# The maxima of the 64-wide attention heads, taken from the high halves of queries and keys as products on half of the array's rows

## The reference

```python
q = (x @ Wq).reshape(b, n, heads, -1)      # 16 heads of 64
k = (ctx @ Wk).reshape(b, j, heads, -1)    # j = 1601 rows of context
v = (ctx @ Wv).reshape(b, j, heads, -1)
sim = jnp.einsum('bihd,bjhd->bhij', q, k) * scale
attn = jax.nn.softmax(sim, axis=-1)
out = jnp.einsum('bhij,bjhd->bihd', attn, v).reshape(b, n, -1)
return out @ Wo + bo
```

## Time and profile before

| | |
|---|---|
| runs | 6561.17, 6562.08, 6566.58 us; median 6562.08 |
| profiled execution | 6568.9 us span, first to last instruction |
| TensorE busy | 6072.1 us, 92% |
| VectorE busy | 4851.4 us, 74% |
| ScalarE busy | 4175.0 us, 64% |
| GpSimd busy | 2747.1 us, 42% |
| mean granted TensorE clock | 0.967 |

### The profile page before, as it was taken

One profiled execution on the slowest core, in us unless ns is written; L12 is line 12 of the kernel. 1 busy time (PEld: TensorE's weight loads), 2 busy tenths in 40 slices (PEclk: granted clock), 3 DMA queues, 4 the chain that ended last, 5 costly groups with the idle time before them and its releaser, 6 DMA issues.

```text
span 6568.9 us, 122562 instructions
## 1 busy us (share of the span) xinstructions
PE 6072.1 (92%) x42376; PEld 3586.6 (55%) x42376; DVE 4851.4 (74%) x9782; ACT 4175.0 (64%) x9228; POOL 2747.1 (42%) x2358
## 2 busy tenths in 40 slices
PE   7999999989899998998989999899898999989988
PEld 5566456654556645664455654566445665456644
DVE  6887776657788777675878877667578886876656
ACT  4556676656655668665765666766575566776656
POOL 3466115751246612564025651266402655126630
PEclk8999999999999999998999999999898999999989
DMA  3111011100111101111011100111001111011100
GB/s 87 36 33 26 22 35 31 28 25 19 48 34 33 27 21 37 30 32 28 13 50 36 33 27 19 38 30 33 23 18 49 31 30 30 16 41 30 28 20 12
DMA packets 347662, 204.18 MB, mean 31 GB/s; under 512 B 165005, under 2 KB 319981, under 8 KB 346926
## 3 DMA queue, kind: packets, MB, share of 16 engines
q1 hardware_dynamic: 347054, 196.34, 11.8%
HBM read 105.18 MB, written 1.05 MB: 16 GB/s over the span
## 4 chain that ended last, share of the span: by engine, by line
PE 73%; DVE 10%; ACT 7%; issue 5%; POOL 4%; SPq 1%; DVEq 0%; DMA 0%; POOLq 0%; ACTq 0%
PE ring L1347 37%; PE o_acc L1347 18%; PE scores L1347 17%; DVE max_part L2097 3%; POOL weight_sum L1309 3%; ACT probs L1782 2%; ACT qop L1636 2%; DVE o_inv L2120 1%; POOL qm L1328 1%; DVE region L2059 1%; DVE qop L2056 1%; ACT qm L1636 1%; DVE ring L2073 1%; PE ring L1451 0%; DVE ring L2076 0%
## 5 line engine op out<-in xcount | busy, mean ns | idle before, releaser
L2097 DVE TENSOR_REDUCE max_part<-ring 128x1 f32<-128x400 f32 (+2 forms) x4608 | 2412.7, 577 | 567.4 <-PE ring L1347 543.8
L1782 ACT ACTIVATE probs<-scores 128x512 f32<-128x512 f32 (+1 forms) x3840 | 2105.9, 599 | 1051.5 <-PE scores L1347 961.8
L1309 POOL TENSOR_TENSOR weight_sum<-weight_sum,probs 128x512 f32<-128x512 f32 (+1 forms) x1408 | 1785.7, 1268 | 201.9 <-ACT probs L1782 66.8
L1347 PE MATMUL o_acc<-probs,region 128*32 128x256 f32 (+2 forms) x13312 | 1348.2, 388 | 11.3 <-ACT probs L1782 6.8
L1636 ACT ACTIVATE region<-ring 64x400 f16<-64x400 f32 (+4 forms) x1744 | 820.4, 480 | 480.6 <-PE ring L1347 291.9
L1309 POOL TENSOR_TENSOR weight_sum<-probs 128x512 f32<-128x512 f32 x256 | 325.4, 1271 | 1619.5 <-PE ring L1347 1194.3
L1347 PEld LDWEIGHTS o_acc<-probs,region 128*32 128x32 f32 (+2 forms) x13312 | 586.0, 122 | 547.0 <-issue 202.4
L1347 PE MATMUL scores<-qop,region 128*128 128x256 f16 (+1 forms) x3328 | 804.1, 274 | 11.3 <-ACT qop L1636 7.8
L1347 PE MATMUL scores<-qop,x_cop 128*128 128x256 f16 (+1 forms) x3328 | 800.1, 273 | 0.0
L1347 PE MATMUL ring<-nk,qm 128*128 128x400 f16 (+2 forms) x2560 | 709.5, 337 | 51.9 <-DVE max_part L2097 19.7
L1347 PE MATMUL scores<-qm,nk 128*128 128x512 f16 (+1 forms) x1920 | 657.3, 389 | 62.1 <-ACT probs L1782 32.0
(11 more groups left out here) (170 smaller groups left out, 7265.9 us busy)
## 6 DMA issues: line engine op xcount, KB each, us to landing
x_cop<-region SPq DMA_DIRECT2D x256, 200.1 KB, 3.1
stage<-in_wide SPq DMA_DIRECT2D x512, 64.0 KB, 2.0
nk<-region SPq DMA_DIRECT2D x192, 100.1 KB, 2.2
stage<-in_wide SPq DMA_DIRECT2D x128, 128.0 KB, 2.6
v_stage<-in_wide SPq DMA_DIRECT2D x256, 64.0 KB, 1.9
wo_stage<-in_wide SPq DMA_DIRECT2D x32, 512.0 KB, 4.0
cop_few<-kop_few SPq DMA_DIRECT2D x256, 32.0 KB, 1.9
ff_w<-in_ff_w SPq DMA_DIRECT2D x24, 256.0 KB, 3.4
```

Of the source, the lines that this page charges most:

```text
L1309: pool.tensor_tensor(total, before, probs[0:rows_, (un.chunk + k) % PROBS, :], ALU.add)\
L1347: return pe.matmul(out, lhs, rhs, start=start, stop=stop, skip_group_check=True)
L1782: act.activation(to, src, ACT.Exp, scale=t.scale).then_inc(exp_done.sem, 1)
L2097: dve.tensor_reduce(dst, src, AX.X, ALU.max).then_inc(*release(one))
```

## The change

Four edits:
1. The maximum products of the wide heads use only the 64 partitions `part` on which both operands hold high halves. Head 0's product lies on rows 0-63 of the array, head 1's on rows 64-127. Each has its own bank.
2. On TensorE such a product no longer waits until the bank of the keys' piece is free (which VectorE's low halves decide) but until ScalarE has written the high half (`op_high`).
3. The planner assumes 0.12 instead of 0.21 for such a job of a cross unit, 0.16 instead of 0.3 for one of a self unit, and the inputs of edit 2.
4. The planner's two groups on TensorE become three: `whole`, `sum` (column parts) and `max` (row halves), with the same `STAY` and 0.1 between any two.

```diff
-def in_tiles(what):
-
-    return what[0] == "values" or what[0] == "job" and UNITS[what[1]].t.jobs[what[2]][0] == "sum"
+def tiling(what):
+
+    if what[0] == "job" and UNITS[what[1]].t.wide and UNITS[what[1]].t.jobs[what[2]][0] in ("max", "sum"):
+        return UNITS[what[1]].t.jobs[what[2]][0]
+    return "sum" if what[0] == "values" else "whole"
...
-            deps = [("DVE", ("job", n, t.jobs.index(("low", k + 1, 0)))), ("DVE", ("job", n, t.jobs.index(("low", 0, 0))))]
-            self.part("PE", "max", due, one, 0.21 if t.cross else 0.3, deps, 0.2)
+            deps = [("ACT", ("job", n, op_job(t, k + 1))), ("ACT", ("job", n, op_job(t, 0)))]
+            self.part("PE", "max", due, one, 0.12 if t.cross else 0.16, deps, 0.2)
...
-                    if e == "PE" and in_tiles(what) != tiled:
+                    if e == "PE" and tiling(what) != tiled:
                         due = due[0] + STAY, due[1]
...
-                    dur += 0.1 * (in_tiles(what) != tiled)
-                    tiled = in_tiles(what)
+                    dur += 0.1 * (tiling(what) != tiled)
+                    tiled = tiling(what)
...
-                        pe.wait_ge(*taken(("job", n, op_job(t, k + 1))))
+                        pe.wait_ge(op_high.sem, op_high.at(n, k + 2))
...
+                        part = slice(64 * h, 64 * h + 64)
                         for m, qq in enumerate(range(QT) if q is None else [q]):
-                            last = mm(out[:, m * w:(m + 1) * w], qop[:, z, h, qq * P:(qq + 1) * P],
-                                      kop_of(un)[:, h, a0:a0 + w], True, True)
+                            last = mm(out[:, m * w:(m + 1) * w], qop[part, z, h, qq * P:(qq + 1) * P],
+                                      kop_of(un)[part, h, a0:a0 + w], True, True)
```

More of the change, by code:

```diff
@@ L672, in run @@
         banks, seen, uses, owner = list(range(RING)), {}, [0] * RING, {}
-        events, now, left, tiled = [], 0.0, len(self.parts), False
+        events, now, left, tiled = [], 0.0, len(self.parts), "whole"
         while left:
```

## The result

The changed kernel takes 6625.79 us (median of 4 runs, 6620.82 to 6630.0), the kernel before 6564.33 us (6561.17 to 6570.43). The ratio is 1.0093, 95% interval 1.0079 to 1.0107: 61 us slower, where +45 was forecast. The profiled executions are 6619.0 and 6568.9 us long, 50 us apart.

What follows compares the result with a forecast made beforehand. TensorE was taken to bound the kernel in cross units. Cross units +56 us, self units 0 and freed waits -11 gave +45: 6562 + 45 = 6607 us, with an 8-in-10 range of 6545 to 6675.

Steps and rivals of the forecast that it cites:

- What bounds the kernel: Wide cross attentions: TensorE sets the time, every chain link on it; in self units a fifth of its time is free.
- The price of a change of use: On TensorE: 0.095 us to enter row halves, 0.10 to leave to float16, 0.195 to float32, 0.14 for column halves.
- What a pair saves: Neighbouring head 0 and head 1 maximum products on different row halves overlap, saving 0.163 us per pair in cross units.
- Sub 1: Wide cross attention: changes of use cost 1.49 us per unit, pairs save 0.98; net +0.51, +33 us over 64 units.
- Sub 7: Wide cross attention: changes of use cost 1.35 us per unit, pairs save 0.98; net +0.37, +23 us over 64 units.
- The freed wait: TensorE no longer waits for VectorE's low halves (21.8 us in 29 waits); 11 us taken back, bounds 0 and 22.
- Self units at 0: Wide self attentions: +17 us of TensorE work, priced at 0 because 19% of its time there is free.
- Rival C: Change costs fall into TensorE's idle time in subs 1 and 7, some 60 us, so time stays at 6565; chance 0.14.

Runs made afterwards that it cites:

- e1: Changed kernel with cross-unit maximum jobs ordered head 0, head 0, head 1, head 1 instead of alternating; 6691.47 us, ratio 1.0194 against the kernel before.
- e8: Kernel before with row halves and their new order in sub 7 alone, but the old wait for VectorE's low halves; 6557.18 us, ratio 0.9992.
- e2: Changed kernel's order on every engine, but maximum products 128 rows deep and waiting for the low halves again; 6669.57 us, ratio 1.0160 against the kernel before.
- e12: Kernel before with row halves, looser wait and new assumed duration in the self units of subs 0 and 6 alone; 6582.95 us, ratio 1.0027.
- e9: Changed kernel with self units of subs 0 and 6 as in the kernel before, row halves only in subs 1 and 7; 6595.74 us, ratio 1.0054.
- e3: Kernel before with the wide heads' maximum products on row halves, its order and waits kept; 6678.46 us, ratio 1.0175.

## Why the prediction was right, point by point

- **What bounds the kernel: right.** The time moved with TensorE's.
- **The price of a change of use: right to 0.01 us.** 0.10 to enter, 0.10 to leave, 0.10 more in front of float32, for 64-row halves as for columns. What the Trainium skill says in TensorEngine Tiling (Array Packing), Tiling Modes, that going over to another tiling mode drains the engine, agrees with the 0.21 between 416.23 and 416.44 where 0.11 is the pace.
- **What a pair saves: nearly right.** 0.14 by e1 against 0.163. The Trainium skill's 3.07 times for four row tiles (TensorE: Matmul & The Clock Gate, Part 3) became 1.5 to 1.8 times for two in the prediction. Its 0.06 to 0.08 are what that saves of one product's 0.17; of a pair's 0.34 the same estimate saves 0.11 to 0.15. So 0.14 agrees with it, and only the 0.163 that the sum used lies a little above.
- **Sub 1: right in the sum, in part by luck.** +33 forecast, +32 measured. Of it the beat has some 0.3 x 64 = 19; the other 13 lie at the seams, where units do not repeat, and nothing was forecast for them. The forecast's beat, 26.4, was 0.15 too high; why is not shown.
- **Sub 7: wrong, the term of +23.** TensorE's work per unit rose much as forecast: 23.01 less the holes of 0.48 is 22.53, and the changed kernel has 22.86, +0.33 against +0.37. But the beat of the kernel before was 23.02, not 22.53: I took "every link of the chain is TensorE" for "TensorE has no holes". The rows said otherwise: 5.4 us idle in 380, and more in the tails of single products, which count as busy. There were 0.48 us of holes per unit; the new order closed the first and the changes of use filled the second. Term: -4 instead of +23.
- **The freed wait: wrong in its place.** The 11 us back stood in no stage, and I expected the wait for low halves to vanish from TensorE. It did not. The changed kernel has

```profile
PE ring L1349 <- DVE region L2062: 20.2, 33, 0.9
```

against 21.8 in 29, since the bank that a low half frees is what any job on `ring` waits for. In sub 7 the looser wait is worth nothing (e8); its worth is in self units, where this order would lose far more without it (e2: sub 0 +71 against +11, sub 6 +27 against -1).
- **Self units at 0: wrong.** 19 by e12, about 25 by e9. The cover of 19% idle time did hide the changes of use in the old order (e3: nothing over the two subs). In the new order it did not hold: TensorE's busy time in the two stages of e12 rose by 17 us, as much as the +17 of work that was counted and priced at 0, and its idle time gave only 5.
- The errors have opposite signs: in the profiled executions sub 7 took 27 us less than forecast, self and narrow stages 22 more, and the 11 us of the wait did not come. That +45 stands near +61 is in part luck; the prices are not. The clock had no term at all, and up to 14 us are its own.
- **Rival C, the cost in waits,** is what happened in sub 7 alone.

What stays open: which moved instructions cost the 19 to 25 us in and around the self units, why TensorE was at the lower clock for 27 us more, and the 4 of 12 us in the narrow stages that lie in subs 4 and 9.

## What to carry to other kernels

Half-array products in pairs are free only when they stand next to each other and to work that already uses another part of the array: count the entries and exits in the order of the instructions, at the price that the trace shows for any change of use, before counting what the pairs save. A static order is made for its assumed waits and durations, so a piece of a change tried in the other's order (e2, e3) measures the misfit too; read such a run by stage. And a chain that runs through one engine does not say that the engine is full: compare the sum of its paces with the beat.

## What the runs showed of the hardware that was not expected

Two float16 products of 400 columns on different row halves, in different banks, last 0.34 us together where one lasts 0.34; two on the same half last 0.51 (e1). A group of projections in float32 that follows another use of the array is 0.10 us longer than the same group behind scores, and pays this beside the 0.10 of the change (1.09 against 0.90, of which 0.10 is the going over to the row halves behind it), which doubles the price of a badly placed visit.
